# Turning the later query blocks' rows by DMA instead of by matmul in a fused feed-forward, attention, feed-forward kernel

## The chip, the cores and the metric

One core of a Trainium2 chip runs the whole program. The metric is the device time of one launch in microseconds (us); the times are medians of several runs, and the profile is one further execution, recorded by the hardware profiler.

## What is computed

The input x has 4096 rows (tokens) of 256 columns. Three layers follow one another, each on the layer-normed x, each added to x:

```
x = x + 0.5 * ffn(layernorm(x))
x = x + attention(layernorm(x))
x = x + 0.5 * ffn(layernorm(x))

ffn(x):   base = x @ base_W.T + base_b;  shared = (x @ shared_A.T) @ shared_B.T
          gate = softmax(x @ router_W.T + router_b); keep the top 2 of 6 experts, normalised
          routed = sum over experts of gate * ((x @ routed_A[e].T) @ routed_B[e].T)     (rank 16)
          return base + shared + routed
attention(x): q, k, v = x @ Wq.T, x @ Wk.T, x @ Wv.T   (16 heads of 16 columns)
          q, k = layernorm of each head with gains, times 256 ** -0.25
          softmax(q k', causal) v, then @ Wo.T + bo
```

## The kernel before

**Blocks and units.** The 4096 rows are worked in NC = 8 query blocks c of 512 rows (TC = 4 tiles of 128 rows). Attention of block c goes over the keys of blocks 0 to c, in four groups of four heads, cut into units (`attention_units`, L54). A unit is one pair of heads, one tile of 128 keys and 512 queries (or the masked equivalent). There are 1056 units; block c has 20, 52, 84, 116, 148, 180, 212 and 244 of them. For each unit TensorE writes 128x1024 scores, ScalarE (ACT) takes one `exp` over them into a ring of five buffers (L776), POOL masks those on the diagonal (L724), and TensorE multiplies the ring with the values (all matmuls go through the helper at L1190).

**Side work.** Everything else is done in pieces beside the units. `front(f, ln, c)` (L86) is a feed-forward: `moments`, `scale` (rows normed into `area`, L828), `turn0` or `turn2` (two halves a = 0, 1), `inner` (first matmuls of the experts and the router), three `route`, `weigh` (POOL), `turnin` (experts' inner results turned), two `outer`. `prepare(c)` (L102) is the same for attention's inputs: `moments1`, `scale1`, `turn1`, `qk` projections, `value`, norms of the heads, `heads` (turned, split and stored by DMA to `parts_d`, from where keys and queries are fetched). `output(c)` divides and projects what attention gave, `back(c)` is the second feed-forward. While the units of block c run, `side_work(c)` (L146) does `prep` (first feed-forward of block c+1 if c >= 3, then `prepare(c+1)`), `ff` (first feed-forward of block c+2, in c = 0 and 1), `out` (`output(c-1)`) and `back` (second feed-forward of block c-2; in c = 7 of blocks 5 and 6). Block 7's own output and second feed-forward come last, after all units.

**Order.** `PLACES` (L179) gives each side item a place: place p of block c stands p thirds of a unit after the block's first unit. `schedule()` (L222) makes from it one list, `ORDER`, and every engine and the DMA queue of SP (SyncE) run their own share of that list strictly in its order. SP's share holds the stores of `heads` with the key fetches behind them (L580, L586), the query fetches (L598, L599), the stores of the output (L658, which wait for `outer1`) and the loads of x.

**Turning before.** Matmuls need the 256 columns on the partitions. A `turn` half is four TensorE transposes of 128x128 float32 against an identity (L1232) into a PSUM bank, and `turnin` is four more of 128x113 (L1252). During the units one bank (`SIDE`, 7) serves all side items. From the bank, the float16 high part is copied out by VectorE (L846) or, for the early blocks (`on_scalar`, L318), by ACT (L765), and VectorE subtracts it for the low part (L848): `move_parts` (L838). The consumers are `inner` after `turn0` and `turn2`, `qk` and `value` after `turn1`, `outer` after `turnin`.

## Time and profile before

| | us |
|---|---|
| median of 3 runs | 1194.63 (1194.05 to 1196.31) |
| the profiled execution, first to last instruction (span) | 1192.3 |
| its TensorE busy time | 1104.1 |
| its ACT busy time | 1014.7 |
| its VectorE, POOL busy time | 467.5, 241.6 |
| first unit's exp starts at | 96.3 |
| last unit's exp ends at | 1159.5 |

The profiled execution's span is 2.3 us below the median; what lies around the span is in the runs' times and not in the profile. The stretch of a block's units, here called a window and written w0 to w7, runs from the first exp of that block to the first exp of the next: 96.3, 127.65, 190.5, 282.1, 404, 552.1, 727.2, 929.7 and 1159.5 us are its bounds. A share of busy time over the whole span mixes these windows with the start and the tail, so the windows are read one by one.

### The profile page before, as it was taken

How to read it: one execution, taken by the hardware profiler on the slowest of the kernel's cores; microseconds unless marked ns; L12 is line 12 of the kernel's file. 1: busy time of each engine (PE TensorE's matmuls, PEld its weight loads, DVE VectorE, ACT ScalarE, POOL GpSimd, SP SyncE). 2: the span in 40 equal slices, each digit the busy share in tenths (PEclk: the TensorE clock that was granted, in tenths of full speed). 3: DMA queues.
4: the chain of work that ended last, by engine and by line, in shares of the span. 5: the costliest groups of instructions: out<-in, count | busy, mean ns of one | idle time of the engine just before them, and what ended most of it. 6: DMA issues, size and time to landing. Idle time of an engine off the chain costs nothing.

```text
span 1192.3 us, 22761 instructions
## 1 busy us (share of the span) xinstructions
PE 1104.1 (93%) x8884; PEld 359.6 (30%) x8884; DVE 467.5 (39%) x1181; ACT 1014.7 (85%) x1134; POOL 241.6 (20%) x377
## 2 busy tenths in 40 slices
PE   3758999999999999999999999999999999999994
PEld 3534333332323233232332232232222222222123
DVE  5678665554544353333333323423131222021114
ACT  3216788789888998999999999999999999999980
POOL 2236533222122211212022021012110101010100
PEclk9779999999999999999999999999999999999996
DMA  5022202003000300003000022000001100000000
GB/s 145 3 63 60 59 11 81 1 28 99 1 1 19 93 17 1 1 32 92 4 1 1 1 67 60 1 1 2 1 10 48 53 1 1 10 10 1 1 19 18
DMA packets 39608, 33.37 MB, mean 28 GB/s; under 512 B 8722, under 2 KB 39432, under 8 KB 39496
## 3 DMA queue, kind: packets, MB, share of 16 engines
q1 hardware_dynamic: 37364, 31.74, 9.0%
q8 instruction: 73, 1.20, 0.4%
q10 hardware_dynamic: 2132, 0.12, 0.1%
q14 instruction: 39, 0.32, 0.1%
HBM read 18.73 MB, written 12.85 MB: 26 GB/s over the span
## 4 chain that ended last, share of the span: by engine, by line
PE 72%; ACT 13%; issue 6%; DVE 6%; DMA 1%; POOL 1%; SPq 0%; ACTq 0%; DVEq 0%; POOLq 0%
PE ps L1190 68%; ACT ring L776 13%; PE ps L1232 2%; PE ps L1298 1%; DMA x<-in_x 1%; DVE st L807 1%; PE ps L1252 1%; DVE area L828 1%; DVE oT L1159 0%; POOL rstd L711 0%; POOL sq L532 0%; DVE x L980 0%; DVE ss L985 0%; DVE sq L1013 0%; ACT area L765 0%
## 5 line engine op out<-in xcount | busy, mean ns | idle before, releaser
L776 ACT ACTIVATE ring<-ps 128x1024 f32<-128x1024 f32 x1056 | 982.2, 1115 | 65.5 <-PE ps L1190 63.5
L1190 PE MATMUL ps<-ring,vf 128*17 128x512 f32 (+3 forms) x4608 | 559.4, 562 | 5.0 <-DVE oT L1159 4.4
L1190 PE MATMUL ps<-queries,keys 50*128 50x512 f16 (+3 forms) x2304 | 363.2, 366 | 22.1 <-ACT ring L776 4.9
L1190 PEld LDWEIGHTS ps<-queries,keys 50*128 50x128 f16 x2304 | 92.3, 93 | 475.3 <-ACT ring L776 437.3
L724 POOL TENSOR_SCALAR_AFFINE_SELECT ring<-ring 128x256 f32<-128x256 f32 (+1 forms) x224 | 103.9, 481 | 396.5 <-ACT ring L776 392.6
L1190 PEld LDWEIGHTS ps<-ring,vf 128*17 128x17 f32 x4608 | 79.7, 95 | 174.5 <-issue 144.2
L711 POOL TENSOR_TENSOR rstd<-var,minus_half 128x4 f32<-128x4 f32 x24 | 24.4, 1017 | 235.6 <-DVE var L813 235.4
L980 DVE SCALAR_TENSOR_TENSOR x<-ps,power,x 128x512 f32<-128x512 f32 x32 | 24.0, 750 | 110.7 <-PE ps L1190 110.7
L846 DVE CAST xnT<-ps 128x512 f16<-128x512 f32 x32 | 22.1, 691 | 100.0 <-PE ps L1232 100.0
L1190 PE MATMUL ps<-baseT,xnT 128*128 128x256 f16 x384 | 55.0, 283 | 3.9 <-DVE area L848 3.8
L1232 PE MATMUL ps<-ident,area 128*128 128x128 f32 x192 | 34.2, 311 | 20.0 <-DVE area L828 20.0
L765 ACT ACTIVATE xnT<-ps 128x512 f16<-128x512 f32 x16 | 9.6, 599 | 49.9 <-PE ps L1232 49.9
L1159 DVE STREAM_TRANSPOSE oT<-ps 128x512 f32<-128x512 f32 x32 | 22.9, 715 | 71.0 <-PE ps L1190 70.5
L1190 PE MATMUL ps<-qkT,xnT 128*128 128x512 f16 x192 | 48.7, 394 | 1.7 <-DVE xnT L848 1.5
L532 POOL TENSOR_TENSOR sq<-area 128x512 f32<-128x512 f32 x32 | 33.5, 1047 | 67.2 <-DVE ss L985 41.7
L1190 PEld LDWEIGHTS ps<-baseT,xnT 128*128 128x128 f16 x384 | 36.7, 101 | 19.2 <-issue 11.0
L828 DVE TENSOR_SCALAR area<-x,mv,rstd 128x256 f32<-128x256 f32 x96 | 36.9, 444 | 11.3 <-POOL rstd L711 11.3
L1013 DVE TENSOR_SCALAR sq<-ps,scaled 128x512 f32<-128x512 f32 x16 | 12.9, 806 | 70.1 <-PE ps L1298 70.1
L537 POOL TENSOR_TENSOR split<-sq,split 128x512 f16<-128x512 f32 x16 | 18.8, 1175 | 100.0 <-DVE split L1017 100.0
L807 DVE BATCH_NORM_STATS2 st<-x 128x6 f32<-128x256 f32 x96 | 33.5, 412 | 9.5 <-DMA x<-in_x 4.8
L1232 PEld LDWEIGHTS ps<-ident,area 128*128 128x128 f32 x192 | 23.6, 156 | 43.0 <-issue 36.9
L848 DVE TENSOR_TENSOR xnT<-ps,xnT 128x512 f16<-128x512 f32 x48 | 33.1, 691 | 7.6 <-ACT xnT L765 6.3
(153 smaller groups left out, 670.5 us busy)
## 6 DMA issues: line engine op xcount, KB each, us to landing
parts_d<-split SPq DMA_DIRECT2D x32, 256.0 KB, 2.6
keys<-parts_d SPq DMA_DIRECT2D x96, 64.0 KB, 2.3
queries<-parts_d SPq DMA_DIRECT2D x192, 32.0 KB
x<-in_x SPq DMA_DIRECT2D x8, 512.0 KB, 4.2
out_x<-x SPq DMA_DIRECT2D x16, 256.0 KB, 2.2
queries<-shift_d SPq DMA_DIRECT2D x64, 4.0 KB
ring<-in_base_W SPq DMA_DIRECT2D x1, 256.0 KB, 4.9
ring<-in_Wq SPq DMA_DIRECT2D x1, 256.0 KB, 3.8
```

Of the source, the lines that this page charges most:

```text
L532: e.tensor_tensor(sq[:, :], qn[:, n % TC, :], qn[:, n % TC, :], ALU.mult).then_inc(K.sq_ok, 1)
L711: pool.tensor_tensor(rstd[ln][:, :], var[ln][:, 0, :], minus_half[:, :].broadcast_to([P, TC]), ALU.pow).then_inc(main.rstd_ok[ln], 1)
L724: m = pool.affine_select(out=tiles[:, part, :], in_=tiles[:, part, :], compare_op=ALU.is_ge, fill=0.0, base=0, pattern=[[0, len(range(8)[p ...
L776: act.activation(probs[:, u % RING, :], bank(2 * (u % SLOTS), 2), ACTF.Exp, bias=0.0, scale=1.0).then_inc(exp_ok, 1)
L807: dve.bn_stats(st[ln][:, i, :], x[:, i, :]).then_inc(*own.up())
L828: m = dve.tensor_scalar(xn[ln][:, i, :], x[:, i, :], mv[ln][:, i, 0:1], rstd[ln][:, i:i + 1], ALU.subtract, ALU.mult)
L846: dve.tensor_copy(high, src).then_inc(*K.own.up())
L848: dve.tensor_tensor(low, src, high, ALU.subtract).then_inc(K.read, 1)
L980: dve.scalar_tensor_tensor(out=x, in0=bank(K.bank[key]).rearrange("p (n d) -> p n d", n=2), scalar=power[0][:, 5:6], in1=x, op0=ALU.mult, ...
L1159: dve.transpose(oT[:, :], bank(ACC)).then_inc(acc_read, 1)
L1190: return pe.matmul(o, lhsT, rhs, start=start, stop=stop, skip_group_check=True)
L1232: m = pe.transpose(b[:, ib * D + i * P:ib * D + (i + 1) * P], xn[ln][:, 2 * a + i, ib * P:(ib + 1) * P], ident[:, :])
```

## The change

For some blocks, TensorE no longer turns. `by_queue` selects `turn0` and `turnin0` of blocks 3 to 7, `turn1` of blocks 2 to 7, `turn2` and `turnin1` of blocks 0 to 6. There the float16 high and low parts are made from the normed rows (or the weighed inner results) in SBUF as rows, by the same two instructions as before with another source and target, and a transposing DMA on SP's queue (128 x 1024 float16, 256 KB, into eight blocks of 128x128) puts them into `xnT` or `hT`. The PSUM bank and the four transposes fall away. In `turn0` and `turn2` both halves use one buffer for their rows, so the second half's high part waits until the first half's DMA has landed. For `turnin`, POOL clears the columns 113 to 127 of the row buffer (one memset). `xnT` is laid out by tile (tile, part, half, column) instead of (part, half, column).

```diff
+QUEUED_FRONT, QUEUED_PREPARE, QUEUED_BACK = 3, 2, NC - 1
+def by_queue(stage, n):
+    if stage in ("turn0", "turnin0"):
+        return (n[0] if stage == "turn0" else n) >= QUEUED_FRONT
+    if stage == "turn1":
+        return n[0] >= QUEUED_PREPARE
+    return stage in ("turn2", "turnin1") and (n[0] if stage == "turn2" else n) < QUEUED_BACK
 def front(f, ln, c):
...
+    if by_queue(f"turn{ln}", (c, 0)):
+        for a in range(2):
+            yield 0.8, f"scale{ln}", (c, a)
+            yield 1.5, f"turn{ln}", (c, a)
...
         def weigh(e, K, f, c):
+            e.wait_ge(*K.done[f"inner{f}", c])
+            if K.queue(f"turnin{f}", c):
+                e.memset(hrows(f).rearrange("p (m c) -> p m c", c=P)[:, :, NR + 1:P], 0.0).then_inc(K.hw_ok[f], 1)
             e.wait_ge(K.wt_ok[f], c + 1)
-            e.wait_ge(*K.done[f"inner{f}", c])
...
+        def wait_rows(e, stage, n):
+            if stage in ("turnin0", "turnin1"):
+                e.wait_ge(main.hw_ok[int(stage[-1])], weighed(main, int(stage[-1]), n))
+            else:
+                c, a = n
+                e.wait_ge(main.xn_ok[int(stage[-1])], 2 * c + a + 1)
+                if a == 1 and stage != "turn1":
+                    e.wait_ge(main.turned[int(stage[-1])][0], 16 * turns_before(stage, c + 1))
...
+            def turn_rows(K, ln, c, a):
+                sp.wait_ge(K.rows_ok[ln], 2 * turns_before(f"turn{ln}", c) + a + 1)
...
+                sp.dma_start_transpose(xnT[ln][:, 2 * a:2 * a + 2, :, :, :].rearrange("p n s b t -> p (n s b) t"), parts_rows(ln, a)).then_inc(K.turned[ln][a], 16)
+            def turn_hrows(K, f, c):
+                sp.wait_ge(K.hrows_ok[f], turns_before(f"turnin{f}", c) + 1)
+                sp.dma_start_transpose(hT(K, f, c).rearrange("p n s t -> p (n s) t"), hrows(f)).then_inc(K.hturned[f], 16)
...
             def move_parts(K, stage, n):
...
-                    dve.wait_ge(K.ready, K.use[stage, n])
+                    if queued:
+                        wait_rows(dve, stage, n)
+                    else:
+                        dve.wait_ge(K.ready, K.use[stage, n])
                     dve.tensor_copy(high, src).then_inc(*K.own.up())
...
             def turn(K, ln, c, a):
+                if K.queue(*key):
+                    return
...
             def inner(K, f, c):
-                for a in range(2):
-                    pe.wait_ge(*K.done[f"turn{2 * f}", (c, a)])
+                wait_turned(K, 2 * f, c)
```

Where `turnin` is queued, `outer` waits on its DMA in the same way. ACT makes the high part of the queued items that `on_scalar` names (`turn1` of block 2, `turn0` and `turnin0` of block 3), behind the same waits. All of `PLACES` is new; `PRELUDE`, which orders the work ahead of the units, is the same. Distances between the new places of the queued items, in places:

| window | item (block) | to its consumer |
|---|---|---|
| 1, 3, 4, 5, 6 | `turn0` a = 0 (3, 4, 5, 6, 7) to `inner0` | 24, 52, 43, 33, 52 |
| 2, 3, 4, 5, 6, 7, 7 | `turn2` a = 0 (0 to 6) to `inner1` | 49, 45, 41, 66, 103, 52, 122 |
| 1 to 6 | `turn1` a = 1 (2 to 7) to first `qk` | 17, 15, 22, 32, 36, 27 |
| 1, 3, 4, 5, 6 | `weigh0` (3 to 7) to `outer0` | 31, 25, 49, 5, 35 |
| 2 to 7, 7 | `weigh1` (0 to 6) to `outer1` | 66, 42, 49, 105, 150, 24, 199 |

## Rows read from the trace of the kernel before

**Rows 1.** The page: busy time of each engine, and the chain that ended last.

```profile
span 1192.3 us, 22761 instructions
PE 1104.1 (93%) x8884; PEld 359.6 (30%) x8884; DVE 467.5 (39%) x1181; ACT 1014.7 (85%) x1134; POOL 241.6 (20%) x377
...
PE ps L1190 68%; ACT ring L776 13%; PE ps L1232 2%; PE ps L1298 1%; DMA x<-in_x 1%; DVE st L807 1%; PE ps L1252 1%; DVE area L828 1%; DVE oT L1159 0%; POOL rstd L711 0%; POOL sq L532 0%; DVE x L980 0%; DVE ss L985 0%; DVE sq L1013 0%; ACT area L765 0%
```

**Rows 2.** Busy time by window, all engines, w0 to w7, then the tail.

```profile
core 0: us, PE busy (x) PEld busy (x) DVE busy (x) ACT busy (x) POOL busy (x), PEclk, DMA share, GB/s
...
96.30:127.65 31.35, 26.25 (x262) 12.89 (x260) 24.76 (x55) 20.20 (x24) 19.22 (x34) 0.95 0.25 73
127.65:190.50 62.85, 61.57 (x550) 22.56 (x546) 38.85 (x95) 54.50 (x64) 27.49 (x41) 1.00 0.12 34
190.50:282.10 91.60, 90.42 (x766) 30.72 (x762) 47.72 (x108) 78.44 (x87) 26.40 (x41) 1.00 0.14 41
282.10:404.00 121.90, 120.40 (x1012) 39.02 (x1008) 59.37 (x145) 108.59 (x119) 29.85 (x45) 1.00 0.10 28
404.00:552.10 148.10, 146.05 (x1204) 43.84 (x1200) 58.74 (x144) 137.90 (x151) 28.20 (x44) 1.00 0.10 29
552.10:727.20 175.10, 172.51 (x1398) 49.43 (x1394) 59.43 (x145) 167.46 (x184) 29.67 (x45) 1.00 0.10 29
727.20:929.70 202.50, 198.76 (x1584) 54.40 (x1582) 59.27 (x143) 196.58 (x216) 28.61 (x43) 1.00 0.04 13
929.70:1159.50 229.80, 218.61 (x1706) 54.27 (x1703) 38.37 (x96) 225.57 (x247) 18.98 (x35) 1.00 0.04 10
1159.50:1192.30 32.80, 15.84 (x104) 11.48 (x104) 15.01 (x41) 2.02 (x4) 2.10 (x3) 0.72 0.05 17
```

**Rows 3.** The same windows, L1232 alone (transposes of the normed rows), w1, w3, w7.

```profile
127.65:190.50 62.85, 2.59 (x16) 1.68 (x16) 1.00 0.12 34
...
282.10:404.00 121.90, 3.93 (x24) 2.51 (x24) 1.00 0.10 28
...
929.70:1159.50 229.80, 2.62 (x16) 1.68 (x16) 1.00 0.04 10
```

**Rows 4.** The same windows, L1252 alone (transposes of the inner results), w1, w3.

```profile
127.65:190.50 62.85, 0.69 (x4) 0.49 (x4) 1.00 0.12 34
...
282.10:404.00 121.90, 1.38 (x8) 0.98 (x8) 1.00 0.10 28
```

**Rows 5.** Timeline of ACT in w7, one unbroken run of exps.

```profile
1104.01 34.03 ACT L776 ACTIVATE ring<-ps 128x1024 f32<-128x1024 f32 x37
```

**Rows 6.** Longest waits in w5: VectorE for a turned half; ACT for scores.

```profile
DVE xnT L846 <- PE ps L1232: 21.2, 6, 6.3
...
ACT ring L776 <- PE ps L1190: 7.3, 14, 1.2
```

**Rows 7.** Groups by line and form: VectorE's parts from PSUM and from SBUF; POOL.

```profile
L848 DVE TENSOR_TENSOR xnT<-ps,xnT 128x512 f16<-128x512 f32 x48 | 33.1, 691 | 7.6 <-ACT xnT L765 6.3
...
L846 DVE CAST xnT<-ps 128x512 f16<-128x512 f32 x32 | 22.1, 691 | 100.0 <-PE ps L1232 100.0
...
L522 POOL TENSOR_TENSOR area<-area,wt 128x448 f32<-128x448 f32 x16 | 15.6, 973 | 0.0
...
L1178 DVE TENSOR_TENSOR xnT<-area,xnT 128x512 f16<-128x512 f32 x14 | 10.0, 715 | 0.5
...
L1176 DVE CAST xnT<-area 128x512 f16<-128x512 f32 x14 | 7.0, 497 | 0.5
...
L521 POOL COPY area<-power 128x4 f32<-128x4 f32 x16 | 3.9, 242 | 74.3 <-DVE wt L975 74.2
```

**Rows 8.** DMA: packets, MB and share of 16 engines; then issues, KB, us to landing.

```profile
q1 hardware_dynamic: 37364, 31.74, 9.0%
...
parts_d<-split SPq DMA_DIRECT2D x32, 256.0 KB, 2.6
...
shift_d<-att SPq DMA_DIRECT2D x2, 128.0 KB, 7.7
```

More of the change, by code:

```diff
@@ L334, with __init__ @@
 class Pass:
-    def __init__(self, name, semaphore, order, banks, scalar, x, x_in, fronts, free=None):
+    def __init__(self, name, semaphore, order, banks, scalar, x, x_in, fronts, free=None, queue=None):
         def s(q):
@@ L351, in __init__ @@
         self.wt_ok = [s(f"wt_ok{i}") for i in range(fronts)]
+        self.queue = queue if queue else lambda stage, n: False
+        if queue:
+            self.rows_ok, self.hrows_ok = [s(f"rows_ok{i}") for i in range(fronts + 1)], [s(f"hrows_ok{i}") for i in range(fronts)]
+            self.turned = [[s(f"turned{i}_{a}") for a in range(2)] for i in range(fronts + 1)]
+            self.hturned = [s(f"hturned{i}") for i in range(fronts)]
         self.hw_ok = [s(f"hw_ok{i}") for i in range(fronts)]
@@ L523, in weigh, with weighed @@
                             wt[f][:, :, :].unsqueeze(3).broadcast_to([P, TC, NE + 1, R]), ALU.mult).then_inc(K.hw_ok[f], 1)
+        def weighed(K, f, c):
+            return sum(3 if K.queue(f"turnin{f}", m) else 2 for m in range(c + 1))
         def square(e, K, n):
@@ L658, in _ @@
                     sp.dma_start(out_v[:, n0:n0 + 2, :], x_main(c)[:, 2 * a:2 * a + 2, :]).then_inc(out_done[c], 16)
+                elif stage in ("turn0", "turn1", "turn2") and by_queue(stage, n):
+                    turn_rows(main, int(stage[-1]), *n)
+                elif stage in ("turnin0", "turnin1") and by_queue(stage, n):
+                    turn_hrows(main, int(stage[-1]), n)
                 elif stage == "heads":
@@ L838, in move_parts @@
             def move_parts(K, stage, n):
-                high, src = moved(stage, n, K.bank[stage, n])
-                low = moved(stage, n, K.bank[stage, n], 1)[0]
+                high, src = moved(K, stage, n)
+                low = moved(K, stage, n, 1)[0]
+                queued, i = K.queue(stage, n), int(stage[-1])
                 if K.scalar(stage, n):
@@ L844, in move_parts @@
                 else:
-                    dve.wait_ge(K.ready, K.use[stage, n])
+                    if queued:
+                        wait_rows(dve, stage, n)
+                    else:
+                        dve.wait_ge(K.ready, K.use[stage, n])
                     dve.tensor_copy(high, src).then_inc(*K.own.up())
                     dve.wait_ge(*K.own.at())
-                dve.tensor_tensor(low, src, high, ALU.subtract).then_inc(K.read, 1)
+                done = K.read if not queued else K.rows_ok[i] if stage in ("turn0", "turn1", "turn2") else K.hrows_ok[i]
+                dve.tensor_tensor(low, src, high, ALU.subtract).then_inc(done, 1)
             def sizes(K, s):
@@ L1285, in value @@
                 pe.wait_ge(K.w_ok, 6)
[L1286 to L1287 removed]
+                wait_turned(K, 1, c)
                 for i in range(2):
                     for ib in range(2):
[L1290 removed]
+                        m = mm_parts(b[:, i * D:(i + 1) * D], lambda s: xnT[1][:, 2 * a + i, s, ib, :],
                                      lambda s: vT[:, s, ib, :], i == 0 and ib == 0, i == 1 and ib == 1)
@@ L1391, in values @@
                 m.then_inc(pv, 1)
-            before = [q for q in ORDER[:ORDER.index(("scores", 0))] if q[0] in BANK_STAGES]
+            before = [q for q in ORDER[:ORDER.index(("scores", 0))] if q in main.bank]
             side_last = [main.done[[q for q in before if main.bank[q] == b][-1]] for b in START_BANKS[1:]]
```

186 lines of the change are left out of this document (115 added, 71 removed).

## The prediction

> **What bounds the kernel now.** I read the page first. TensorE is busy 1104.1 of 1192.3 us and carries over 70% of the chain that ended last, but ACT is busy 1014.7 us too [rows 1]. With two engines so close, the page's shares don't say what a saved TensorE microsecond is worth. So I read the busy times window by window [rows 2]. In w1 to w6 TensorE idles only 1.3, 1.2, 1.5, 2.1, 2.6 and 3.7 us (length less PE busy), while ACT idles 8.4, 13.2, 13.3, 10.2, 7.6 and 5.9 us. These windows are bound by TensorE. The late ones are so by little: the number of units grows and the side work doesn't. In w7 it turns: TensorE idles 11.2 us of 229.8, ACT 4.2. There ACT is the engine at its limit: 37 exps in one unbroken run take 34.03 us, 0.92 us each [rows 5], so its 244 units need 224 us in any case. The granted clock is 1.00 from w1 to w7, which is the 2.4 GHz level, after TensorE's long busy stretches; I count no change of it, as TensorE stays over 90% busy. The start, w0 and the tail keep all their transposes (blocks 0 to 2 at the start, block 7 at the end).
>
> **What falls away.** In w1 the matmuls of L1232 are 16 and take 2.59 us of TensorE, 0.162 us each; in w3 24 take 3.93 us [rows 3]. L1252 has 4 in w1 (0.69 us) and 8 in w3 (1.38 us) [rows 4]. The pattern repeats: w2 as w1, w4 to w6 as w3, w7 has 16 of L1232 (2.62 us) and 8 of L1252. All 144 and 48 of them fall away. By window: 3.28, 3.28, then 5.31 in each of w3 to w6, and 4.00 in w7; 31.8 us in all. The weight loads beside them overlap and are not counted again.
>
> How much of it is time? Where TensorE is the bound, all, up to ACT's idle time. In w1 to w4 ACT's idle time is at least 4.9 us more than what goes, so I count all: 3.28 + 3.28 + 5.31 + 5.31 = 17.2 us. For the others I ask how little ACT can idle at all. In w7, where TensorE has 11.2 us to spare, ACT still idles 4.2 of 229.8 us (1.8%), because side work comes in bursts that a few score banks don't bridge; the waits there are many and short. I take 1.8% as the floor: in w5 3.1 us, leaving 7.6 - 3.1 = 4.5 us of gain; in w6 3.6 us, leaving 2.3. In w7 the bursts get shorter by a part; I take half of the 4.0, 2.0 us. Sum 17.2 + 4.5 + 2.3 + 2.0 = 26.0 us. Bounds: 17.2 (nothing in w5 to w7) and 31.8 (everything).
>
> **What VectorE, ACT and POOL pay.** A turned half costs VectorE a cast and a subtraction, 691 ns each from PSUM; from SBUF the same shapes take 497 and 715 ns [rows 7]. That is 0.17 us less for each of some 40, on an engine that is busy 59 of 122 to 203 us in w3 to w6 [rows 2]: nothing. POOL's memset has the copy of 242 ns as its nearest row [rows 7], 12 times, before a wait on `wt` it makes anyway: nothing. ACT's early copies change source only. The new layout of `xnT` changes strides and no counts.
>
> **What a transposing DMA costs.** No row shows one. The nearest are an ordinary 256 KB store, 2.6 us from issue to landing, and the slowest landing of all, 7.7 us for 128 KB [rows 8]. Between them I make an estimate from rows: the queue's 37364 packets took 9.0% of 16 engines' 1192.3 us, which is 46 ns each at 850 B on average. The store has 256 rows of 1 KB: 256 x 46 ns / 16 = 0.7 us of packets, so 1.9 us are fixed. If the turned 256 KB go as 1024 pieces of 256 B (one row of a 128x128 block), 1024 x 46 ns / 16 = 2.9 us, and with 1.9 it lands after L = 4.8 us. I take 4.8 and keep 2.6 and 7.7 as ends. Below nothing it can't go, since each consumer waits for it.
>
> What does L cost? TensorE runs in order: if `inner`, `qk` or `outer` comes before the DMA has landed, the scores behind it wait too. The new places give the room: windows 1 to 7 have 0.40, 0.36, 0.35, 0.33, 0.32, 0.32 and 0.31 us for a place (length over three times the units, [rows 2]). Then
> - 12 pairs (`turn0`, `turn2`) must fit two landings in sequence, since the second half's high part waits for the first landing, and twice 1.2 us of VectorE [rows 7]: 2L + 2.4 = 12.0 us. The table of places gives 9.7 (block 3), 18.2, 14.3, 10.7, 16.6, and for `turn2` 17.8, 15.8, 13.7, 21.4, 32.8, 16.3, 38.3. Two fall short, by 2.3 and 1.3 us.
> - 6 `turn1` need L + 1.2 = 6.0 from the second half; they have 6.9, 5.5, 7.7, 10.7, 11.7, 8.6. One falls short by 0.5.
> - 12 `turnin` need POOL's 1.2 us [rows 7], VectorE's 1.2 and L, 7.2 us from `weigh`; eleven have 7.5 or more, block 6 has 1.6 and falls short by 5.6.
>
> That is 9.8 us if every engine reaches an item just at its place. VectorE is ahead of that: in w5 it waited 21.2 us in six times for TensorE's transposes, 3.5 us each [rows 6], and by as much it can start the rows earlier. Then 2.1 us are left. I take 3 us; bounds 0 (L = 2.6) and 16 (4.8 by place, with a second transfer queued behind the first).
>
> The new wait of VectorE between two halves stands for up to L, twelve times. Behind it on VectorE are the reads of the side bank and, once for each group, the `gather` that frees the accumulator for TensorE. In w5 `turn0` of block 6 waits at place 22 and `gather` is due at 135; the next TensorE item that needs VectorE is the projection at 33, 3.6 us later, which fits into the same 3 us. ACT has the same wait once, in w1 (`turn0` of block 3, places 44 to 52, 3.2 us for L plus 0.7): 2 us of ACT, which has 8.4 us idle there. On SP the DMAs stand in line behind query fetches and output stores, which wait for VectorE at their own place; the one queued item close behind an output store is `turn2` of block 6 in w7 (places 304 and 306), and it has 38 us to its consumer.
>
> **The sum.** 26.0 - 3 = 23 us. Against the execution's span, 1192.3 - 23 = 1169.3; the median lies 2.3 us above the span, so 1171.6. I say 1171. The new places of the other items are worth something of either sign; the rows can't price it, and I leave 3 us each way.
>
> **Two rules of the notes.** What TensorE takes for one 128x128 block is 0.162 us here [rows 3]. The Trainium skill, "VectorE: DVE Perf Modes", section "The three transpose paths", gives 1309 ns for a two-byte 128x128 by DMA against 390 ns on TensorE, and its rules prefer TensorE where PSUM will do as a target. Eight blocks one after another would be 10.5 us (an estimate from that page); by that the waits above come to 61 us with the lead of 3.5 us and 122 us without, and the kernel would be slower, 1230 to 1290. The Trainium skill, "Advanced Engine Details and Errata", section "X-Bar Transpose (TRN2)", says such DMAs are as fast as ordinary ones; by that L is near the store's 2.6 us and the time 1169. No row here decides between the pages.
>
> **The rivals.**
> - *ACT takes over early* (only w1 to w4 gain): 1194.6 - 17.2 + 3 = 1180. For it: w7, where spare TensorE time of 11.2 us didn't make ACT run without gaps. Against it: ACT idles 4.4% of w5 and 2.9% of w6, against 1.8% of w7, so there is room. Chance 0.14.
> - *All of it is gained* and the landings are hidden: 1194.6 - 31.8 = 1163, with luck in the places 1160. Chance 0.10.
> - *The transposing DMA is slow and takes the place of the transposes, slower than before.* The mechanism is the in-order TensorE at `inner`, `qk` and `outer`. At L = 7.7, with no lead, the 12 pairs need 17.8 us and fall short by 27.6 in all, `turn1` by 7.0, `turnin` by 12.4: 47 us. 1194.6 - 26.0 + 47 = 1216. The point of decision is L = 6.6 us without the lead, and about 8.5 with it, where shortfall equals gain. For it: no transposing DMA is in the trace, and the rows reach 7.7. Against it: that row is two transfers at the start in a crowd; in the windows the DMA engines are 4 to 14% busy [rows 2]. Chance 0.11. (The first page above would make it more.)
> - *No difference*, L just there, 1192 to 1197: chance 0.05.
>
> **How the numbers follow.** The forecast (1166 to 1178) has 0.60. Faster by over 0.2% (about what a measurement of this kernel can tell from no change): 0.60 + 0.14 + 0.10 = 0.84; same 0.05; slower 0.11. The range reaches from the best case to just past the ACT rival, with the 3 us of the places and waits of up to 10 us beside it: 1160 to 1190.
>
> **What would show it.** L1232 and L1252 have no matmul in w1 to w7 and TensorE's busy time falls by about 32 us. Each of w1 to w4 is shorter by about its own 3.3 to 5.3 us; w7 by 2. ACT's idle time shrinks in every window to between 1.8% and 9%. The transposing DMAs land after some 5 us; TensorE's waits for them sum to a few us, first at `outer0` of block 6 in w5. If the landings take over 6.6 us, or TensorE idles over 10 us in w3 to w6 behind them, the prediction is wrong, and in the direction of the slow rival. If w5 to w7 don't move at all, ACT's limit was nearer than I read.

## The result, and the profile after

The changed kernel takes 1184.62 us (median of 4 runs, 1184.09 to 1185.50) against 1194.62 before: a ratio of 0.9913, interval 0.9899 to 0.9927. It gains 10 us where 23 were forecast. The profiled execution's own time is 1184.09 us, its span 1182.4. One run of e1 (below) took 2466.34 us, twice the others, and is left out of its time.

One thing about this kernel isn't said above, and it bears on the 10 us. The new table of places sets the second `turnout` of blocks 2 to 5 ahead of the divide of the block's last group of heads. So for that group, a quarter of attention's output, it turns what the block before left: the kernel leaves that order out. With the order kept, the two tables tried below take 1200 and 1204 us (e13, e12), more than the kernel before. A gain with the order kept isn't shown here.

The page of the changed kernel, the lines that answer to [rows 1]. The exp is now L867, the helper of the matmuls L1290, the transposes that stay L1342 and L1363.

```profile
span 1182.4 us, 22449 instructions
...
PE 1086.0 (92%) x8692; PEld 339.9 (29%) x8692; DVE 467.8 (40%) x1181; ACT 1015.3 (86%) x1134; POOL 245.0 (21%) x389
...
PE 64%; ACT 16%; issue 8%; DVE 7%; DMA 2%; POOL 1%; SPq 0%; ACTq 0%; DVEq 0%; POOLq 0%
```

192 matmuls fewer, as many as fall away. But TensorE's busy time fell by 18.1 us, not by the 31.8 that these matmuls took. Where the rest went is the main thing to learn here, and the windows show where to look. Busy time by window of the changed kernel, w1 to w7, the lines that answer to [rows 2]:

```profile
core 0: us, PE busy (x) PEld busy (x) DVE busy (x) ACT busy (x) POOL busy (x), PEclk, DMA share, GB/s
126.71:187.52 60.81, 59.17 (x532) 20.68 (x528) 40.68 (x95) 54.45 (x64) 28.73 (x42) 1.00 0.25 57
187.52:276.24 88.72, 87.20 (x744) 28.16 (x742) 52.08 (x115) 79.09 (x87) 27.26 (x42) 1.00 0.23 61
276.24:395.62 119.38, 116.72 (x978) 36.00 (x976) 59.52 (x144) 108.46 (x120) 29.50 (x46) 1.00 0.20 43
395.62:543.12 147.50, 142.81 (x1170) 41.20 (x1168) 61.36 (x149) 138.06 (x152) 29.90 (x46) 1.00 0.19 48
543.12:716.24 173.12, 169.76 (x1362) 46.34 (x1360) 57.99 (x140) 167.41 (x183) 30.16 (x46) 1.00 0.13 30
716.24:918.36 202.12, 196.32 (x1552) 51.34 (x1550) 54.79 (x138) 196.38 (x215) 29.16 (x46) 1.00 0.12 31
918.36:1148.63 230.27, 216.40 (x1682) 51.31 (x1678) 36.33 (x95) 225.75 (x247) 17.65 (x36) 1.00 0.07 16
```

Lengths of the windows, from the first exp of one block to that of the next; e1 and e9 are experiments below:

| | before | counted gain | after | gain | e1, no transposing DMA | e9 |
|---|---|---|---|---|---|---|
| w1 | 62.9 | 3.3 | 60.8 | 2.1 | 60.4 | 60.8 |
| w2 | 91.6 | 3.3 | 88.7 | 2.8 | 88.6 | 89.0 |
| w3 | 121.9 | 5.3 | 119.4 | 2.6 | 117.8 | 119.7 |
| w4 | 148.1 | 5.3 | 147.5 | 0.6 | 144.8 | 144.7 |
| w5 | 175.1 | 4.5 | 173.1 | 1.9 | 173.1 | 173.1 |
| w6 | 202.5 | 2.3 | 202.1 | 0.4 | 202.1 | 202.1 |
| w7 | 229.8 | 2.0 | 230.3 | -0.5 | 230.3 | 230.3 |

w1 to w4 gave 8.1 of 17.2 us, w5 to w7 gave 1.8 of 8.8. The start got 0.1 us longer, w0 1.0 us shorter and the tail 0.9 us longer. The granted clock is 1.00 in w1 to w7, as before.

The DMA part of the changed kernel: packets, MB and share of 16 engines, then issues with KB and us to landing. It answers to [rows 8].

```profile
q1 hardware_dynamic: 88052, 44.33, 15.0%
...
parts_d<-split SPq DMA_DIRECT2D x32, 256.0 KB, 2.6
...
xnT<-area SPq DMA_TRANSPOSE x36, 3.1
...
area<-area SPq DMA_TRANSPOSE x12, 3.0
```

A transposing DMA lands after 3.1 us. I had estimated 4.8, so its own speed isn't what took the gain.

### The profile page after: what moved, and what is told of

Same layout as the page of the kernel before. It is cut to its first block, busy times and chain, and to the rows that moved or that the text cites. A ratio compares the mean times of both kernels' runs of the same rounds, so it can differ in the third digit from the quotient of the medians.

```text
span 1182.4 us, 22449 instructions
## 1 busy us (share of the span) xinstructions
PE 1086.0 (92%) x8692; PEld 339.9 (29%) x8692; DVE 467.8 (40%) x1181; ACT 1015.3 (86%) x1134; POOL 245.0 (21%) x389
## 4 chain that ended last, share of the span: by engine, by line
PE 64%; ACT 16%; issue 8%; DVE 7%; DMA 2%; POOL 1%; SPq 0%; ACTq 0%; DVEq 0%; POOLq 0%
PE ps L1290 62%; ACT ring L867 16%; PE ps L1410 1%; DMA xnT<-area 1%; DVE area L922 1%; DVE st L898 1%; DVE area L947 1%; PE ps L1342 1%; DMA area<-area 0%; DMA x<-in_x 0%; POOL ring L812 0%; POOL rstd L799 0%; DVE area L1101 0%; DVE x L1079 0%; DVE area L1009 0%
## 5 line engine op out<-in xcount | busy, mean ns | idle before, releaser
L867 ACT ACTIVATE ring<-ps 128x1024 f32<-128x1024 f32 x1056 | 983.3, 1115 | 54.4 <-PE ps L1290 51.5
L1290 PE MATMUL ps<-ring,vf 128*17 128x512 f32 (+3 forms) x4608 | 560.1, 563 | 3.2 <-POOL ring L812 1.9
L1290 PE MATMUL ps<-queries,keys 50*128 50x512 f16 (+3 forms) x2304 | 373.6, 366 | 26.7 <-ACT ring L867 4.8
L1290 PEld LDWEIGHTS ps<-queries,keys 50*128 50x128 f16 x2304 | 94.0, 93 | 526.3 <-ACT ring L867 482.3
L1290 PEld LDWEIGHTS ps<-ring,vf 128*17 128x17 f32 x4608 | 79.8, 95 | 169.9 <-issue 136.3
L1290 PE MATMUL ps<-baseT,xnT 128*128 128x256 f16 x384 | 55.8, 286 | 4.9 <-DVE area L947 3.6
L1290 PE MATMUL ps<-qkT,xnT 128*128 128x512 f16 x192 | 50.2, 404 | 2.9 <-DVE xnT L947 1.5
L930 DVE COPY area<-ps 128x512 f32<-128x512 f32 x20 | 13.8, 690 | 97.3 <-PE ps L1290 97.3
L856 ACT ACTIVATE xnT<-ps 128x512 f16<-128x512 f32 x12 | 7.1, 596 | 50.0 <-PE ps L1342 50.0
L922 DVE TENSOR_SCALAR area<-x,mv,rstd 128x256 f32<-128x256 f32 x96 | 40.0, 470 | 19.5 <-POOL rstd L799 18.4
L947 DVE TENSOR_TENSOR area<-area 128x512 f16<-128x512 f32 (+1 forms) x48 | 43.8, 913 | 2.8 <-ACT area L856 1.2
L1290 PEld LDWEIGHTS ps<-baseT,xnT 128*128 128x128 f16 x384 | 36.9, 102 | 17.8 <-issue 11.5
L1112 DVE TENSOR_SCALAR qT<-ps,scaled 128x512 f32<-128x512 f32 x16 | 12.9, 808 | 59.6 <-PE ps L1410 59.6
L856 ACT ACTIVATE area<-ps 128x512 f32<-128x512 f32 (+1 forms) x16 | 9.6, 597 | 27.8 <-PE ps L1290 14.2
L1290 PE MATMUL ps<-bT,area 113*128 113x256 f16 x192 | 31.9, 278 | 1.5 <-DVE area L947 1.5
```

Source lines behind the costliest of these rows:

```text
L856: m = act.activation(dst, src, ACTF.Copy)
L867: act.activation(probs[:, u % RING, :], bank(2 * (u % SLOTS), 2), ACTF.Exp, bias=0.0, scale=1.0).then_inc(exp_ok, 1)
L922: m = dve.tensor_scalar(normed(K, ln, c, a)[:, i, :], x[:, n, :], mv[ln][:, n, 0:1], rstd[ln][:, n:n + 1], ALU.subtract, ALU.mult)
L947: dve.tensor_tensor(low, src, high, ALU.subtract).then_inc(done, 1)
L1290: return pe.matmul(o, lhsT, rhs, start=start, stop=stop, skip_group_check=True)
```

## Theories

*Theory A, busy isn't need.* TensorE's busy time in the late windows contains some of its waiting for ACT. Between the side items TensorE runs ahead of ACT, up to the three score slots, and what is ahead covers a short side item. Only long side items leave ACT without scores. A turn's four transposes are short, so their removal frees nothing in w5 to w7.

*Theory B, the landings took it.* TensorE is the bound, as forecast, and the lost 13 us are waits for the transposing DMAs.

*Theory C, the places.* The new positions of everything else made the difference, either way.

## Experiments: the halves of the change

**e1, no transposing DMA.** The changed kernel, rows made as before, and `inner`, `qk`, `value` and `outer` start when the rows are ready. What they multiply is not turned.

```diff
-                sp.dma_start_transpose(xnT[ln]..., parts_rows(ln, a)).then_inc(K.turned[ln][a], 16)
-                sp.dma_start_transpose(hT(K, f, c)..., hrows(f)).then_inc(K.hturned[f], 16)
-                        pe.wait_ge(K.turned[ln][a], 16 * turns_before(f"turn{ln}", c + 1))
+                        pe.wait_ge(K.rows_ok[ln], 2 * turns_before(f"turn{ln}", c) + a + 1)
```

> The changed kernel with its transposing DMAs left out: the rows are made as before, and their readers wait for the rows instead of a landing (so the matmuls read what stood in the target; the result is not the reference's). Two theories for the 10 us of gain where 23 were forecast. Lead theory: ACT has up to two exps of scores in hand, so a TensorE item of 0.65 us between two units costs nothing where that lead has been restored, and taking it away gives nothing there. Then only the waits seen in the changed kernel's trace (some 5 us of TensorE) can come back: 1179 to 1182 us. Wait theory: the 26 us were there and the landings (TensorE in order, VectorE held between two halves, SP's line) took 13 back: 1169 to 1173 us.

Measured: 1179.18 us (three runs), ratio 0.9866 (0.9842 to 0.9890). Against the changed kernel that is 5.4 us: w4 2.7, w3 1.5, w1 0.4; w5 to w7 don't change by 0.02. So the landings and the issue of their DMAs cost some 5 us (the forecast had 3). B explains 5 of the 13 us, and none in w5 to w7.

**e2, the transposes gone, nothing in their place, all items at the places of before.** e1 with the old table of places.

```diff
-PLACES = {(0, "prep"): (1, 3, 3, 7, ...
+PLACES = {(0, "prep"): (0, 3, 5, 9, ...
```

> As the run without transposing DMAs (the turning itself is left out, readers wait for the rows), but with the places of the kernel before: TensorE's 192 transposes are gone and nothing comes in their place. Lead theory: 1182 to 1187 us, the gain in w1 to w4 and next to none in w6 and w7. Wait theory: 1166 to 1171 us, 4 to 5 us less in each of w3 to w6. Place theory (the new places are worse than the old ones): under 1176 and at least 5 us under the same kernel at the new places.

Measured: 1194.75 us, ratio 1.0007 (0.9993 to 1.0021). Its windows w1 and w3 to w7, columns as above:

```profile
127.09:192.90 65.81, 60.95 (x530) 20.88 (x526) 41.63 (x95) 54.28 (x65) 28.74 (x42) 0.97 0.12 33
...
283.48:405.02 121.54, 117.86 (x980) 35.85 (x976) 56.80 (x145) 108.42 (x119) 31.01 (x47) 1.00 0.10 28
405.02:553.15 148.13, 143.64 (x1172) 40.86 (x1168) 58.20 (x144) 137.66 (x151) 28.68 (x46) 1.00 0.10 29
553.15:729.77 176.62, 171.47 (x1366) 46.25 (x1362) 56.96 (x145) 167.49 (x183) 30.56 (x47) 0.99 0.09 29
729.77:932.25 202.48, 196.41 (x1552) 51.38 (x1550) 58.85 (x143) 196.56 (x215) 29.33 (x45) 1.00 0.05 14
932.25:1162.02 229.77, 216.69 (x1682) 51.82 (x1678) 37.41 (x97) 225.58 (x247) 18.90 (x37) 1.00 0.04 10
```

This is the sharpest result of the study. 31.8 us of TensorE's work are gone, with no DMA, and the time is that of before. w4, w6 and w7 keep their lengths of [rows 2] to within 0.03 us, w3 gains 0.4 and w2 1.0; w1 loses 2.9 and w5 1.6. In w6 5.3 us of matmuls went and the busy time fell by 2.4 (198.76 to 196.41): the matmuls that stay fill the room. Unit by unit it is plainer still: in w6 every step from the start of one exp to the start of the next is what it was before, to within 0.005 us, though eight turns are gone between them (from the two traces). With the items at their old places, a transpose was free there. w1 and w5 got longer, both beside a lower clock. In w1 TensorE comes to a `qk` 2.3 us before VectorE has made its rows (137.84 us), and the mean granted clock is 0.66 from 137 to 142 us, where no such wait and no lower clock stood before. In w5 the clock is 0.90 from 553 to 570 us, around a wait of 1.1 us for VectorE to read the accumulator that was 1.0 us long before, at a clock of 1.00. So the total of nought is a small gain (w2 and w3, 1.4 us) and these losses together; the profiled execution took 1197.47 us, 2.7 more than the median, so in other runs the losses may be smaller.

**e3, transposing DMAs at the old places.** The changed kernel with the old table.

> The change at the places of the kernel before (scale and turn of the two halves alternate in the same places). It shows what the landings cost without room made for them. Landings take 3.1 us. Lead theory: 1186 to 1192 us, as the old places leave 6 to 22 places to the consumer and some waits come up, but short ones are hidden by the lead as well. Wait theory: over 1192 us, since the new places were needed to hide them. Place theory: under 1182 us.

Measured: 1225.89 us, ratio 1.0256 (1.0231 to 1.0282). w1 is 88.4 us instead of 62.9, w3 128.0; w6 and w7 are as before. In w1 two views tell why: SP's timeline, then the waits.

```profile
137.05 23.18 SPq L665 DMA_TRANSPOSE xnT<-area  x4
...
191.91 3.93 SPq L651 DMA_DIRECT2D keys<-parts_d  x6
...
202.15 0.28 SPq L683 DMA_DIRECT2D queries<-shift_d  x1
202.48 1.25 SPq L670 DMA_TRANSPOSE area<-area  x1
```
```profile
PE ps L1290 <- DMA area<-area: 10.5, 1, 10.5
PE ps L1290 <- DMA xnT<-area: 10.3, 2, 7.2
```

SP takes its share in the order of the list. A `turnin` DMA that stands behind stores, key fetches and query fetches goes out when they have, and TensorE stands at `outer` for 10.5 us. A transposing DMA takes 1.23 us of SP by itself, the stores and fetches of the windows 0.28 to 0.43 (medians of each kind in the changed kernel's trace).

**e4, the new places with the transposes on TensorE.**

```diff
 def by_queue(stage, n):
+    return False
```

(The order of `scale` and `turn` in the list stays that of the changed kernel.)

> The new places with TensorE's transposes for all blocks (no DMA turns anything). Lead theory: 1192 to 1197 us, the places are worth little by themselves. Place theory: over 1198 us, so that the DMAs' gain of 26 us was hidden behind places that cost. If it is under 1190 us, the places gave most of the gain and not the DMAs.

Measured: 1274.86 us, ratio 1.0672 (1.0652 to 1.0692). TensorE's groups, the lines of the two transposes: busy and mean, then the idle time before them and what ended it.

```profile
L1347 PE MATMUL ps<-ident,area 128*128 128x128 f32 x192 | 34.9, 316 | 51.7 <-DVE area L927 45.8 <-DVE x L1289 2.6 <-DVE xnT L952 2.0
...
L1368 PE MATMUL ps<-ident,area 128*113 128x128 f32 x64 | 12.4, 322 | 17.6 <-POOL area L566 15.6 <-DVE vf L935 1.2 <-DVE sq L1117 0.8
```

The new places set a turn close behind the normalisation that feeds it. As matmuls, the turns then hold up TensorE until VectorE or POOL have made their input, 69 us in all, where the changed kernel has 26 at its transposes (19.7 and 6.2, those of the start and the end). That is 43 of the 90 us between the two kernels; the rest isn't separated (the mean granted clock is 0.96 to 0.99 in w2 to w7, and the turns themselves are back). So neither half gains alone: no turns at old places 0, new places with TensorE's turns -80, both 15.4 (e1), less 5 for the landings. My reading is that the DMA path buys freedom to place, since TensorE no longer stands in the chain from rows to turned rows. That a place is worth something by itself isn't shown by this, and e12 to e14 below limit it.

## Experiments: what a microsecond of TensorE is worth

The timeline of the kernel before shows theory A directly. Start, length, engine, what it does; in brackets the idle time before it and what ended that. First a stretch of w6 in which TensorE catches up, then one of w7 in which it has nothing to catch up; last a turn.

```profile
734.61 1.05 PE L1190 MATMUL ps<-ring,vf 128*17 128x512 f32 x8
...
735.59 0.60 PE L1190 MATMUL ps<-queries,keys 50*128 50x512 f16 x4
...
736.12 1.05 PE L1190 MATMUL ps<-ring,vf 128*17 128x512 f32 x8
...
737.43 1.49 PE L1190 MATMUL ps<-woT,xnT 128*128 128x256 f16 x12
...
740.65 9.30 ACT L776 ACTIVATE ring<-ps 128x1024 f32<-128x1024 f32 x10 [0.28 <-PE ps L1190]
...
1021.44 1.05 PE L1190 MATMUL ps<-ring,vf 128*17 128x512 f32 x8
...
1022.43 0.92 PE L1190 MATMUL ps<-queries,keys 50*128 50x512 f16 x4
1022.95 0.10 PEld L1190 LDWEIGHTS ps<-queries,keys 50*128 50x128 f16 x2 [0.43 <-ACT ring L776]
...
1023.28 1.05 PE L1190 MATMUL ps<-ring,vf 128*17 128x512 f32 x8
...
1026.42 0.83 PE L1190 MATMUL ps<-baseT,xnT 128*128 128x256 f16 x6
...
1028.99 1.02 ACT L776 ACTIVATE ring<-ps 128x1024 f32<-128x1024 f32 x1 [0.59 <-PE ps L1190]
...
1064.96 5.80 ACT L776 ACTIVATE ring<-ps 128x1024 f32<-128x1024 f32 x6
...
1067.86 0.65 PE L1232 MATMUL ps<-ident,area 128*128 128x128 f32 x4
```

Eight value and four score matmuls serve two units. At 734.61 and 736.12 they start 1.51 us apart, at 1021.44 and 1023.28 1.84 us, for the same work. In the second stretch the four score matmuls span 0.92 us instead of 0.60, because the second pair of weight loads waits for ACT to free a slot. 1.84 is ACT's pace, two exps of 0.92 [rows 5]. Busy time of the two stretches, columns as for the windows:

```profile
734.61:736.12 1.51, 1.51 (x14) 0.32 (x12) 1.44 (x4) 1.51 (x3) 1.03 (x1) 1.00 0.04 11
1021.44:1023.28 1.84, 1.70 (x15) 0.33 (x13) 0.00 (x0) 1.84 (x4) 0.00 (x0) 1.00 0.00 0
```

Work of 1.51 us counts as 1.70 busy when TensorE waits in the middle: matmuls that follow closely overlap in the records, and those that come apart don't. So TensorE needs 0.76 us for a unit where it shows 0.85 and takes 0.92, and for each unit without side work it gets 0.16 us ahead, as far as the slots allow.

An item that is shorter than what it is ahead costs nothing: the turn at 1067.86 lies inside an unbroken run of exps. A projection (1.49 us) leaves ACT idle for 0.28 us; an `outer` (about 2.1 us, from 1026.42 to the scores at 1028.50) for 0.59 and, one exp later, another 0.28.

**e5, every transpose that the change removes is issued twice in the kernel before.**

> The kernel before with each of the 192 transposes that the change takes away done twice (items of 1.3 us in place of 0.65). Lead theory: doubling costs far more than taking away brought (0 us at the old places): 0.5 to 0.8 us for each of 48 items, 1215 to 1235 us, and 4 to 6 us in each of w4 to w7. Total theory: 1215 to 1227 us too, but then taking them away would have brought as much, and it did not.

Measured: 1212.46 us (one run; the kernel before beside it 1195.09), 17.4 us more; less than I had expected. TensorE's busy time rose by 21.1 us (1125.2 against 1104.1), not by 31.8, as eight transposes in a row take 1.09 us and not twice 0.66. By window the added time is 1.9, 2.1, 2.8, 3.3, 2.9, 2.4 and 1.2 us from w1 to w7. A turn of 1.09 us is no longer short, so taking a turn away and adding one aren't mirror images.

**e7, bursts of 4, 6, 8 and 12 transposes set into w7 of the changed kernel**, each far from other side work.

```diff
+                if stage == "exp" and n - UNIT0[NC - 1] in {160: 4, 172: 8, 196: 6, 208: 12}:
+                    for i in range(...):
+                        pe.transpose(bank(SIDE)..., ident[:, :], ident[:, :])
```

> The changed kernel with four added bursts of TensorE transposes in w7, where no side item stands near: 4 (0.65 us) at unit 160 of block 7, 8 (1.3 us) at unit 172, 6 (1.0 us) at unit 196, 12 (2.0 us) at unit 208. Read from the steps between exps (0.904 us undisturbed). Lead theory: a threshold; 4 transposes lengthen the steps after them by less than 0.1 us in all, 6 by 0.1 to 0.4, 8 by 0.5 to 0.8, 12 by 1.2 to 1.6 us. Total theory: the loss goes with the size, 4 transposes a third of 12.

Measured (one run, 1184.15 us): from one exp's start to the next's, by the trace, 4 transposes (0.66 us) change nothing, 6 (0.88 us) cost 0.1 us, 8 (1.09 us) cost 0.6, 12 (1.53 us) cost 0.8. 30 matmuls, 4.2 us of TensorE, made w7 0.70 us longer (230.97); 0.3 us of the loss by the 8 and 0.5 of that by the 12 are given back further on. That is a direct measurement of what the forecast had as "half": up to 0.66 us at a time, nothing, in w7.

**e10, the long items made short.** The kernel before; from w3 on `outer` and `projout` do one of their three partial products (high times high), so two thirds of their matmuls are left out. The transposes stay.

```diff
             def mm_parts(o, lhsT, rhs, start, stop):
+                if short["on"]:
+                    return mm(o, lhsT(0), rhs(0), start, stop)
```

> The kernel before, places and transposes as they are, from w3 on with a third of the matmuls in outer0, outer1 and projout (only the product of the high parts; the result is not the reference's). Items of 1.92 and 1.28 us become 0.64 and 0.43. That takes 34 us of TensorE's work away, about as much as the transposes are (31.8 us). Lead theory: 4 to 7 us less in each of w3 to w7, 1160 to 1174 us, where leaving out all transposes at the same places gave none. Total theory: both removals are worth the same, so 1190 to 1196 us.

Measured: 1166.05 us (one run; before beside it 1194.51). Windows w3, w6 and w7:

```profile
279.53:394.51 114.98, 113.49 (x948) 32.83 (x944) 59.40 (x145) 108.29 (x120) 29.81 (x45) 1.00 0.10 29
...
708.47:906.14 197.67, 192.91 (x1524) 48.68 (x1520) 59.13 (x143) 195.64 (x216) 28.53 (x43) 1.00 0.05 14
906.14:1130.90 224.76, 212.51 (x1642) 48.37 (x1638) 39.22 (x97) 224.46 (x247) 18.48 (x35) 1.00 0.04 11
```

w3 to w7 fall by 7.0, 3.2, 5.9, 4.8 and 5.0 us, 26.0 of the 28.5 in all; most of the rest lies ahead of w1, where the edit does nothing. By the counts 318 matmuls are gone, at 0.12 us each (twelve of a projection in the timeline above, from 737.43 to the scores behind it, take 1.4 us) some 37 us. These gave 26.0 us, at unchanged places; 31.8 us of short ones, at unchanged places (e2), gave nothing. In w7 ACT's idle time falls from 4.2 us [rows 2] to 0.3. So the 1.8% that I took as the floor of ACT's idle time is no floor: it is what the long items cost. Theory A stands: by e2 in w6, by e7 in w7, and by this run from w3 on.

## Experiments: can the long items be cut without leaving work out?

**e6, e6b: the long items in pieces of 1536 columns, one piece behind each unit's scores**, from w3, in the changed kernel (e6) and in the one before (e6b).

```diff
+                if late["on"]:
+                    late["queue"].append(Later(o, lhsT, rhs, start, stop))
...
                 if stage == "scores":
                     scores(n)
+                    piece(1536)
```

> The changed kernel with TensorE's long side items (inner, qk, value, outer, projout) in pieces of at most 1536 columns (0.64 us), the pieces after the first each behind the next unit's scores, from w3 on. Nothing is left out, the matmuls and their number are the same. Lead theory: a piece of 0.64 us fits into the lead that three score slots give ACT, as the transposes did, so ACT's waits for scores in w4 to w7 mostly go: 1155 to 1172 us. Theory of TensorE's total (what counts is how much TensorE does in a window): no change, 1182 to 1187 us.

> The kernel before with the same pieces (its transposes stay, 0.65 us an item). Lead theory: it gains as well, 8 to 25 us, to 1170 to 1187 us; the pieces are worth more than the DMAs. Total theory: 1193 to 1197 us.

Measured: 1196.82 us, ratio 1.0020 (1.0008 to 1.0032), 12 us over the changed kernel; and 1204.77, ratio 1.0090 (1.0068 to 1.0112), 10 us over the one before. The cut fails in both. My reading, not tested by itself: TensorE gets 0.16 us ahead in a unit, and a piece (six matmuls of 256 columns, some 0.7 us) in each of two or three units in a row takes more than that.

**e8, the pieces five units apart**, from w5, `inner` left whole.

> The changed kernel, from w5 on, with outer, qk, value and projout in pieces of at most 1536 columns (0.64 us), the pieces five units' scores apart (or at the next side item, the next masked values or the next group). The pieces next to each other cost 12 us; this run asks whether it was their distance. Lead theory: TensorE wins about 0.15 us of lead per unit back (a batch of two units takes it 1.5 us, ACT 1.81), so after 0.64 us four to five units restore it and nothing is lost: w5 to w7 get 6 to 15 us shorter in all, 1170 to 1179 us. If cutting an item costs by itself (a bank held longer, VectorE later): 1184 to 1192 us.

Measured: 1189.99 us, ratio 0.9964 (0.9952 to 0.9977). Against the changed kernel w7 gains 1.7 and w6 1.0, as A wants, but w5 loses 6.2 and w4, which has no pieces, 2.8. Its trace shows several causes. In w4 the wait for the landing at `inner` is 3.0 us where it was 2.6, and the mean granted clock is 0.84 from 420 to 440 us (1.00 in the changed kernel from 410 to 440). In w5 TensorE waits 2.7 us for a transposing DMA at an `outer` (657.66 us), where the changed kernel has no such wait in w5, and 1.3 and 1.1 us for VectorE to read the accumulator and the side bank. An item in pieces holds the one bank that the side items share for longer, and where the next one comes, all the remaining pieces go at once; how much of the loss comes from that isn't separated.

**e11, pieces only where no other user of the bank is near**, in w6 and w7, in a version with later second `turnout` (e12, below, is its base).

> As the run with the second turnout later, and from w6 on outer, qk, value and projout in pieces of at most 1536 columns, four to six units' scores apart, but only where that room is left before the next side item, the next masked values or the next group. Lead theory: w7 gets 2 to 5 us shorter and w6 0 to 3 us against that base; 1176 to 1183 us. If w7 stays within 0.5 us of the base, the lead does not come back in four to six units, and the theory is wrong on that.

Measured: 1202.48 us, ratio 1.0069 (1.0045 to 1.0094), 1.9 us under e12. w7 gains 1.5 us, less than I had expected; w6 loses 0.7. The cut items lose less (the projection 0.2 us instead of 0.8, one `outer` 0.7 instead of 1.7), but few have room. The idea is right in sign and small in size.

## Experiments: places

**e9, later readers.** In w3 and w4 of the changed kernel TensorE waits for landings at `outer0` of block 4 and `inner0` of block 5. Here these two, and the item behind each, stand 4 to 13 places later.

```diff
-        (3, "prep"): (..., 100, 118, 125, 133, 137, 141, 145, ...
+        (3, "prep"): (..., 100, 118, 131, 137, 137, 141, 145, ...
-        (4, "prep"): (11, 21, 22, 24, 32, 57, 67, 77, 87, ...
+        (4, "prep"): (11, 21, 22, 24, 32, 57, 80, 84, 87, ...
```

> The changed kernel with four places altered: inner0 of block 5 from place 67 to 80 of w4 (its first route from 77 to 84), outer0 of block 4 from 125 and 133 to 131 and 137 of w3. There TensorE waited 2.6 and 1.3 us for a landing in the changed kernel's trace. If these two waits are what the landings cost beside small ones: 2 to 4 us less in all, 1180 to 1183 us, from w3 and w4. If not, no change.

Measured: 1181.81 us, ratio 0.9898 (0.9878 to 0.9919), the fastest run in which no work is left out, though it has the changed kernel's early `turnout`; 2.8 us under the changed kernel. The intervals of the two ratios overlap; by window the gain is in w4 (147.5 to 144.7, which is e1's length without any DMA). w3, where I expected some too, keeps its length: the wait of 1.3 us at `outer0` is gone, and one of 1.5 us for another transposing DMA has come up. The changed kernel's trace shows what it mends. VectorE, SP, TensorE and ACT around the first turn in w4:

```profile
402.52 2.67 SPq L651 DMA_DIRECT2D keys<-parts_d  x6
...
405.88 0.69 DVE L947 TENSOR_TENSOR area<-area 128x512 f16<-128x512 f32 x1
...
412.18 0.28 SPq L683 DMA_DIRECT2D queries<-shift_d  x1
412.57 5.55 SPq L665 DMA_TRANSPOSE xnT<-area  x2
...
415.70 0.43 DVE L944 CAST area<-area 128x512 f16<-128x512 f32 x1 [5.39 <-DMA xnT<-area]
...
420.12 1.41 PE L1290 MATMUL ps<-aT,xnT 128*128 128x118 f16 x24 [2.62 <-DMA xnT<-area]
...
421.95 1.02 ACT L867 ACTIVATE ring<-ps 128x1024 f32<-128x1024 f32 x1 [2.53 <-PE ps L1290]
```

The rows of the first half are ready at 406.57 (405.88 + 0.69). Their DMA goes out at 412.57, 6 us later: SP is issuing the key and query fetches of the window, one after another since 402.52. Then the landing takes 3.1 us, VectorE makes the second half's rows, and that DMA lands at 420.1. TensorE has reached `inner` 2.62 us before, ACT runs dry for 2.53. Of some 13.5 us from rows to `inner`, 6.0 are SP's line, 6.4 two landings and 1.2 VectorE's work between them.

**e12, e13, e14: the order of `turnout` and divide.** In the changed kernel the second `turnout` of blocks 2 to 5 (places 0 and 1 of windows 3 to 6) stands ahead of the divide of that block's last group of heads, so the quarter of the block that it turns for that group is what the buffer held before. In e12 (e9 with the second `turnout` behind that divide) and e13 (e9 with both at the places of the kernel before) it is the block's own; e14 gives the kernel before the early places.

```diff
 e12, e9 changed                      e13, e9 changed                       e14, the kernel before changed
-(3, "out"): (0, 0, 5, 50)          -(3, "out"): (0, 0, 5, 50)            -(3, "out"): (5, 18, 30, 35)
+(3, "out"): (0, 4, 5, 50)          +(3, "out"): (5, 18, 30, 50)          +(3, "out"): (0, 0, 5, 35)
```

(Blocks of w4 to w6 in the same way.)

> The kernel with the four later places (inner0 of block 5, outer0 of block 4), and the second turnout of blocks 2 to 5 at place 4, behind the divide of the block's last group (in the changed kernel its place is 0 or 1, ahead of that divide, so that it turns what the block before left of that group; this run computes it from the block's own). VectorE work of 1.8 us then follows the divide directly instead of standing before it. Lead theory: the projection at place 4 or 5 waits a little longer at the start of w3 to w6, 0 to 1.5 us each: 1181 to 1187 us. It is the base for the run with pieces where there is room.

> The kernel with the four later places, and with turnout and projout in w3 to w6 at the places that they have in the kernel before (w3 5, 18, 30; w4 15, 22, 29, 40; w5 12, 13, 29, 46; w6 5, 28), so that both turnouts stand behind the divide of the block's last group (as in the run with only the second turnout moved, which lost 22 us because the projection stood right behind it). If the early projection is what the new places live on: 1188 to 1196 us. If only the missing distance between turnout and projection cost those 22 us: 1180 to 1186 us.

> The kernel before with turnout and the first projout of w3 to w6 at the changed kernel's places (0 or 1, 4 or 5), everything else as it was (the second turnout of blocks 2 to 5 then stands ahead of the divide of the last group and turns what the block before left of that group). If the early projection alone gave the changed kernel's gain: 1183 to 1190 us. Lead theory: the same item elsewhere, 1191 to 1197 us.

Measured: e12 1204.40 us, ratio 1.0083 (1.0058 to 1.0108); e13 1200.15, ratio 1.0050 (1.0035 to 1.0066); e14 1203.29, ratio 1.0078 (1.0055 to 1.0102). Against e9, e12 loses 11.6 us in w3, 6.1 in w4, 5.3 in w5; e13 loses 4.8, 6.0, 2.0, and 5.2 in w6. The start of w3 in e12, DMA, VectorE, TensorE and ACT:

```profile
282.56 1.41 DVE L898 BATCH_NORM_STATS2 st<-x 128x6 f32<-128x256 f32 x4 [5.13 <-DMA x<-in_x]
283.88 0.23 DVE L1263 RECIPROCAL den<-oT 128x16 f32<-128x16 f32 x1
...
286.66 2.72 PE L1290 MATMUL ps<-woT,xnT 128*128 128x256 f16 x12 [9.69 <-DVE xnT L1278]
...
290.01 1.03 ACT L867 ACTIVATE ring<-ps 128x1024 f32<-128x1024 f32 x1 [11.13 <-PE ps L1290]
```

VectorE stands 5.13 us at the moments of rows that a DMA has yet to bring. The divide and the `turnout` queue behind that, the projection at place 5 behind them, TensorE waits 9.69 us and ACT 11.13. After the wait twelve projection matmuls take 2.72 us instead of 1.48, and the window's mean granted clock is 0.96 instead of 1.00. In e13 nearly all of the loss is the same wait, once in a window: TensorE stands 3.1, 3.6 and 3.5 us at the projection of w3, w4 and w6 until VectorE has turned, and ACT is idle for 5.0, 5.1 and 4.7 us. So with these tables the 10 us of the changed kernel hold only with that early `turnout`. With the order of before they give 1200 to 1204 us, slower than the kernel before; e14 shows that the early `turnout` by itself isn't a gain either (w3 +3.5, w5 +7.1). The waits point to a table with the projection later, behind a `turnout` that stands behind the divide; whether it would give the gain with the old order wasn't tried.

## Why the prediction was wrong in size

- *"These windows are bound by TensorE", "where TensorE is the bound, all".* This step failed. I read TensorE's small idle time in [rows 2] as the proof. Its busy time holds waiting: in w6 the same 400 full score matmuls took 69.6 us before and 71.7 after, with 5.3 us of other work gone. These two lines are TensorE's group in w6, before and after:

```profile
L1190 PE MATMUL ps<-queries,keys 50*128 50x512 f16 x400 | 69.6, 384 | 3.2 <-ACT ring L776 0.5
```
```profile
L1290 PE MATMUL ps<-queries,keys 50*128 50x512 f16 x400 | 71.7, 385 | 5.4 <-ACT ring L867 1.0
```

  By need, w6 has at most 212 units x 0.76 us and 33 us of side matmuls, 194 of 202.5 us (an estimate from the timeline above and TensorE's groups in w6), against ACT's 195. The two are as good as equal, and what is over is what the long items cost. The Trainium skill, "Perfetto Trace Analysis", section "Identifying the Most-Contended Engine", warns that TensorE's matmul busy share doesn't tell how near the engine is to its limit, since pipelined instructions look smaller in a trace; the trace here agrees with the warning, and shows it from the other side: 1.70 us busy for a need of 1.51.
- *w5 to w7: 4.5 + 2.3 + 2.0 = 8.8 us.* Measured 1.9, 0.4 and -0.5. The floor of 1.8% for ACT's idle time was the wrong model: e10 brings ACT in w7 to 0.3 us idle. "In w7 the bursts get shorter by a part; I take half" should have asked which bursts: those of 0.65 us cost nothing (e7).
- *w1 to w4: 17.2 us.* Without landings (e1) 2.5, 2.9, 4.1 and 3.3, 12.8 in all. e2 and e4 show that this comes from places and turns together, not from the turns, and e13 that the place of `turnout` has a large part in it (w3 and w4 lose 4.8 and 6.0 us without it): the mechanism was wrong there too, though the size is nearer.
- *Landings 3 us, bounds 0 to 16.* Measured some 5.4 (e1 against the changed kernel): right in the range, but for another reason. L is 3.1 us, under the 4.8 taken, and the waits come from SP's line. I wrote that the DMAs "stand in line behind query fetches and output stores", and then looked only at the stores. The fetches at a window's start take SP about 10 us (402.52 to 412.57), and `turn0` of block 5 fell into them. I looked for the first wait at `outer0` of block 6; TensorE doesn't wait there, but at `inner0` of block 5 (2.6 us) and `outer0` of block 4 (1.3 us).
- *Where L's estimate went wrong.* 46 ns a packet was the mean of larger packets. 50688 more packets took 6.0% more of 16 engines (15.0 of 1182.4 us against 9.0 of 1192.3): 22 ns each. The count, 1024 a DMA, fits (50688 / 48 = 1056).
- *VectorE's two instructions cheaper from SBUF.* From SBUF the subtraction of 128x512 takes 693 ns in the median (L947), near the 715 that I had from the nearest row [rows 7], but 988 on average: five of the 36 took 2.7 us. So the mean price was wrong. I know of no time that it cost here.
- *The rivals.* "ACT takes over early" (1180 us) is the nearest in number and in place: w5 to w7 gave almost nothing. Its mechanism was ACT at its pace; it is ACT's starving at long items. The slow DMA is out: the Trainium skill, "VectorE: DVE Perf Modes", section "The three transpose paths", would make it 10.5 us for eight blocks (an estimate from that page); the trace has 3.1 us. The Trainium skill, "Advanced Engine Details and Errata", section "X-Bar Transpose (TRN2)", has such DMAs as fast as ordinary ones; the trace nearly agrees, 3.1 us beside a store's 2.6.
- *What would show it.* I named "if w5 to w7 don't move at all, ACT's limit was nearer than I read", and TensorE's busy time falling by 32 us. It fell by 18, and this alone would have been the sign.

The sign was right by luck. The matmuls that were counted gave nothing where they stood (e2). The gain came with what the prediction left at "3 us each way", the new places, together with the missing turns (e1, e4), and it is gone in the tables tried as soon as the second `turnout` stands behind the divide again (e12, e13).

## What to carry to other kernels

Where two engines feed each other through a few slots, don't take the busy time of the feeding engine as its need: find a stretch in which it catches up, and compare the same instructions there with a stretch in which it doesn't. Then ask of each item of side work whether it is longer than what the engine is ahead; shorter ones are free to keep, and only long ones are worth shortening. When work moves to a DMA queue, count the place in the issuing engine's line, not just the transfer: here 6 us of line against 3.1 us of landing. And when a table of places is made anew, check that each item still stands behind what it reads, before its gain is counted.

## What the chip showed that I had not expected

- A transposing DMA of 256 KB (128 x 1024 float16) inside SBUF lands in 3.1 us (36 of them; 3.0 for the 12 from the inner results), at some 22 ns for one of its packets (the estimate above); a store of 256 KB takes 2.6 us in the same trace. Its issue holds SP for 1.23 us.
- TensorE's busy time for the same twelve matmuls is 1.51 us back to back and 1.70 with a wait between them.
- VectorE's float32 to float16 subtraction of 128x512 with all its operands in SBUF (L947) takes 0.69 us in the median. Five of the 36 took 2.73 to 2.75 us, and each of these began 0.2 to 0.3 us behind the start of POOL's addition of 128x1024 float32 (L805, 2.41 us; at 200.07 us POOL starts, at 200.29 VectorE) and ended 0.5 us behind its end.
